# A fifth input tile of a routed convolution kernel: four block products, or three

## Chip, cores, metric

One core of one Trainium2 chip runs the kernel. The metric is the device time of one execution in microseconds (us), the median of several runs; lower is better.

## The reference

A grouped convolution of length 9 with a bias per sample and channel, then a router that picks 16 of 64 experts per row, and a low-rank layer whose 512 inner columns are weighted by the router:

```
h = conv1d(x, weight, pad 4, groups 4) + (c @ c_weight.T)[:, :, None] + bias     # x is (32, 64, 1024)
scores = (h @ Wq.T) @ keys.T                      # 64 scores of a row of 1024
gate = softmax of the 16 largest scores, 0 elsewhere
z = h @ A.T                                       # 512 = 64 experts x 8
out = x + 2.0 * (z * gate, expert by expert) @ B.T
```

## The kernel before

The 2048 rows are cut into 16 tiles of 128 rows: four tiles to each of the four channel groups, and eight samples to a tile. The program is written engine by engine. Each engine runs its own list of steps in the order of the code, and semaphores are the only thing that ties the lists together.

Every float32 product is made of three products of rounded parts. An operand has a high half (rounded, made on ACT by `high`, L509) and a low half (the rest, a subtraction on DVE by `low`, L1102, or in a few cases on GpSimd): high x high + high x low + low x high. A matmul of 512 columns is one TensorE instruction.

A tile t goes through these steps.

- Its input block is loaded (`load_blocks`), split into `x_hi` and `x_lo` (`split_x`), and convolved on TensorE into `p_conv`. The first five tiles (t < TW = 5) use the direct form, `conv` at L866: two output halves, two input blocks each, three products each, 12 matmuls. From tile TW on, the two halves share a product. DVE forms two differences of input blocks (`differ`, L1126), ACT splits the wider block of 1536 columns, TensorE makes 3 matmuls with the summed weights `ws` (`conv_sum`), ACT adds the bias and spreads the result over both halves in PSUM (`add_u_shared`, L559), and TensorE adds 3 matmuls to each half (`conv_pair`): 9 matmuls in all. `sum_w` and `split_ws` make the summed weights and their halves, once per channel group.
- ACT adds the bias (`add_u`, eight instructions, one a sample, into `h_c`) in the direct form. DVE transposes the rows into `h_t` (`turn_h`), and ACT and DVE split them (`split_h`: `h_hi`, `h_lo`).
- `z_product` multiplies by A and the query weights: 48 matmuls of 264 columns into two PSUM banks, `p_z` (tile 1: `p_out`). ACT takes the query (`take_q`), TensorE turns it, ACT copies it back (`copy_q`), TensorE makes the scores.
- DVE selects: `copy_scores`, `top_first`, `take_first`, `top_second`, `take_second`, `weigh`, `invert`, then `gate` in two instructions, which empties the banks of `p_z`, and `turn_z`. The gated z goes through DRAM and comes back transposed. `split_z` makes `zt_hi` and `zt_lo`.
- `out_high` (high and low z with `b_hi`) and `out_low` (high z with `b_lo`) make the output product, 24 matmuls of 512 columns for a tile, DVE adds x, and SP stores.

The weights B come in four chunks, c = 0 to 3. ACT makes `b_hi` of each, DVE the low halves of 1 to 3, and GpSimd that of 0 in four pieces of 256 columns (L499). `b_lo_done(c)` says which semaphore stands for a low half.

Buffers tie the steps together as well. While t < TW, the blocks lie in three slots of 1032 columns; later in two slots of 1544, over the same memory. So `load_blocks(t)` waits for the split of the tile that lay there. `x_hi`, `x_lo`, `h_hi` and `h_lo` have two slots each. `z_product(3)` needs the banks of `p_z`, so it waits for `gate(2)`.

The change touches the stretch from 22 to 50 us. TensorE finishes tile 2's z product and scores there, convolves tile 4 (L785), makes the output product of tile 0 (L933, L934, L941), and begins tile 3's z product (L892). The four lists were written out by hand for the first tiles, one call a line.

Of the kernel before, what the change touches and what calls it, by code (L numbers as in the profile page):

```python
# [14 lines left out]


NT = 16
TW = 5
TS = 4
FP = 6  # L20
NP = (NT - 2 - FP) // 2
# [24 lines left out]
def adaln_ffn(nc, x_blocks, x_rows, conv_w, a_wq, b_w, small, out):  # L46
# [13 lines left out]
    with ExitStack() as ctx:  # L60
# [197 lines left out]
        BP = 4  # L258
# [2 lines left out]
            return (s_wlop, 1) if g == 1 else (s_wlo, max(g, 1))  # L261

        def b_lo_done(c):
            return (s_blo, c) if c else (s_blop, BP)

        def x_lo_done(t, half=1):
            return s_xlo, x_split_count(t, half)
# [207 lines left out]
        @block.gpsimd  # L475
        def _(pool):
            nc.gpsimd.memset(ones, 1.0).then_inc(s_ones, 1)
            nc.gpsimd.memset(ident[:], 0.0).then_inc(s_iz, 1)
            nc.gpsimd.memset(q_w[:], 0.0).then_inc(s_qz, 1)
            nc.gpsimd.memset(q_t[:].bitcast(F32), 0.0).then_inc(s_qtz, 1)  # L480
            pool.wait_ge(s_iz, 1)
            nc.gpsimd.affine_select(out=ident[:], in_=ident[:], compare_op=ALU.not_equal, fill=1.0, base=0,
                                    pattern=[[-1, P]], channel_multiplier=1).then_inc(s_ident, 1)

            pool.wait_ge(s_cw, 1)
            nc.gpsimd.tensor_copy(cw[:, 2:NG], sm[:, SMALL_CW + 2 * CI:SMALL_CW + NG * CI].rearrange("d (g c) -> d g c", c=CI)
                                  .unsqueeze(2).to_broadcast([P, NG - 2, R, CI])).then_inc(s_cw, 1)

            pool.wait_ge(s_a[A_POOL], 16)
            nc.gpsimd.tensor_copy(a_hi[:, A_POOL, :], a_raw[:, A_POOL, :]).then_inc(s_ahp, 1)  # L490

            def split_w(g):
                pool.wait_ge(s_whi, g + 1)
                nc.gpsimd.tensor_tensor(w_lo[:, g % 2], w_raw[:, g], w_hi[:, g % 2].bitcast(F32), ALU.subtract).then_inc(s_wlop, 1)

            def split_b(c, piece):
                cols = slice(piece * L // BP, (piece + 1) * L // BP)
                pool.wait_ge(s_bhi, c + 1)
                nc.gpsimd.tensor_tensor(b_lo[:, c, cols], b_raw[:, c, cols], b_hi[:, c, cols].bitcast(F32),  # L499
                                        ALU.subtract).then_inc(s_blop, 1)  # L500

            split_w(1)
            for piece in range(BP):
                split_b(0, piece)

        @block.scalar
        def _(act):
# [65 lines left out]
            def split_b(c):  # L573
                act.wait_ge(s_b[c], 16)
                high(b_hi[:, c, :], b_raw[:, c, :], s_bhi)
# [79 lines left out]
            def copy_q(i):  # L655
                act.wait_ge(s_qtp, i + 1)
                high(q_f[:], p_conv[:, 2, 0:P], s_qt)
# [42 lines left out]
            add_u(3)  # L700
            exp(0)
            split_h(2)
            split_x(4)
            split_keys()
            take_q(1)
            split_w(1)
            copy_q(1)
            split_b(0)
            split_b(1)
            take_q(2)  # L710
            exp(1)
            copy_q(2)
            split_h(3)
            split_z(0)
            split_b(2)
            split_b(3)
            add_u(4)
            exp(2)
            sum_w(1)
            split_x(5)  # L720
            take_q(3)
            split_z(1)
# [53 lines left out]
        def _(pe):  # L776
# [89 lines left out]
            def conv(t):  # L866
                conv_direct(t, (0, 2, 1))
# [170 lines left out]
            z_product(2, 1, (0,), range(R // 2, R))  # L1038
            z_product(2, 2, (0,), range(R))
            scores(2)  # L1040
            conv(4)
            out_high(0, 0)
            out_high(0, 1)
            out_low(0, 0)
            out_low(0, 1)
            for i in range(3, NT):
# [53 lines left out]
        def _(dve):  # L1100
# [265 lines left out]
            gate(0)  # L1366
            turn_z(0)
            split_h(2)
            split_x(4)
            turn_h(3, 0)  # L1370
            turn_h(3, 1)
            copy_scores(1)
            top_first(1)
            take_first(1)
            top_second(1)
            split_b(1)
            take_second(1)
            weigh(1)
            invert(1)
# [11 lines left out]
            weigh(2)  # L1391
            invert(2)
            gate(2)
            sum_w(1)
            differ(5, 0)
            differ(5, 1)
            split_ws(1)
            turn_z(2)
            turn_h(4, 0)
            turn_h(4, 1)  # L1400
# [162 lines left out]
```

## Time and profile before

| | us |
|---|---|
| median of 3 runs (227.99 to 228.99) | 228.86 |
| profiled execution | 228.66 |
| its span, first to last instruction | 226.9 |
| TensorE busy with matmuls | 222.9 |
| DVE busy | 194.5 |
| ACT busy | 126.4 |
| GpSimd busy | 7.6 |

The span is what the trace covers; 1.8 us of the profiled execution lie around it. Busy time is a sum over instructions. Instructions of one engine overlap a little at their ends, so the time between two starts is the better measure of what one costs. All stamps below are us from the start of the span.

### The profile page before, as it was taken

To read this page: it belongs to the slowest core of one execution; us is meant where nothing else is said; L and a number is where in the kernel's file an instruction comes from. 1 tells how busy PE (TensorE), PEld (TensorE's weight loads), DVE (VectorE), ACT (ScalarE), POOL (GpSimd) and SP (SyncE) were. 2 spreads that over 40 slices of the span, in tenths; PEclk is the share of its full clock that TensorE was granted. 3 is DMA by queue.
4 is the path that set the end of the run, shared out by engine and by line. 5 is a ranking of instruction groups with operands and counts; after the bars stand their busy time and mean duration, and the time that the engine had idled before them with its cause. 6 is when DMAs were issued, how large, how long until landed. Compare 5 with 4: busy or idle time off the path is not lost.

```text
span 226.9 us, 4036 instructions
## 1 busy us (share of the span) xinstructions
PE 222.9 (98%) x1351; PEld 198.4 (87%) x1351; DVE 194.5 (86%) x443; ACT 126.4 (56%) x317; POOL 7.6 (3%) x16
## 2 busy tenths in 40 slices
PE   8999999999999999999999999999999999999995
PEld 6889998898988989889989889898998989898884
DVE  1799889999999989999999999899989995868442
ACT  4898857357274592936473856648473853252200
POOL 2010053000000000000000000000000000000000
PEclk9999999999999999999999999999999999999999
DMA  6997048659864666545261616655472337157642
GB/s 199 371 401 313 4 111 286 215 181 288 290 209 103 207 210 181 182 131 201 85 196 47 185 28 186 207 139 189 131 249 85 114 120 248 43 161 256 198 162 95
DMA packets 24869, 40.89 MB, mean 180 GB/s; under 512 B 2832, under 2 KB 11920, under 8 KB 24848
## 3 DMA queue, kind: packets, MB, share of 16 engines
q1 hardware_dynamic: 24704, 40.55, 55.4%
q8 instruction: 11, 0.18, 0.3%
q10 hardware_dynamic: 144, 0.08, 0.2%
q14 instruction: 10, 0.08, 0.1%
HBM read 28.04 MB, written 12.58 MB: 179 GB/s over the span
## 4 chain that ended last, share of the span: by engine, by line
PE 94%; DVE 3%; issue 1%; ACT 0%; POOL 0%; DVEq 0%; POOLq 0%
PE p_z L892 36%; PE p_conv L841 9%; PE p_out L933 6%; PE p_out L934 6%; PE p_out L941 6%; PE p_conv L785 5%; PE p_out L892 3%; PE p_out L961 3%; PE p_out L965 2%; PE p_out L963 2%; PE p_t L961 2%; PE p_conv L961 2%; PE p_t L963 2%; PE p_conv L965 2%; PE p_conv L963 2%; PE p_t L965 2%
## 5 line engine op out<-in xcount | busy, mean ns | idle before, releaser
L509 ACT ACTIVATE h_hi<-h_t 128x1024 fp32r<-128x1024 f32 x16 | 17.1, 1069 | 36.3 <-DVE h_t L1144 36.3
L892 PEld LDWEIGHTS p_z<-a_hi,h_hi 128*128 128x128 f32 x240 | 32.6, 188 | 2.1 <-DVE a_hi L1156 0.2
L892 PE MATMUL p_z<-a_hi,h_hi 128*128 128x264 f32 x240 | 34.2, 285 | 0.0
L892 PE MATMUL p_z<-a_hi,h_lo 128*128 128x264 f32 x240 | 34.1, 284 | 0.0
L892 PE MATMUL p_z<-a_lo,h_hi 128*128 128x264 f32 x240 | 33.9, 284 | 0.0
L892 PEld LDWEIGHTS p_z<-a_hi,h_lo 128*128 128x128 f32 x240 | 31.3, 188 | 0.2
L892 PEld LDWEIGHTS p_z<-a_lo,h_hi 128*128 128x128 f32 x240 | 31.0, 188 | 0.0
L1102 DVE TENSOR_TENSOR x_lo<-x_blk,x_hi 128x1536 fp32r<-128x1536 f32 (+4 forms) x18 | 25.3, 1406 | 2.3 <-ACT x_hi L509 2.2
L933 PE MATMUL p_out<-b_hi,zt_hi 128*128 128x512 f32 (+1 forms) x64 | 25.0, 393 | 0.0
L934 PE MATMUL p_out<-b_hi,zt_lo 128*128 128x512 f32 (+1 forms) x64 | 24.7, 388 | 0.0
L559 ACT ACTIVATE p_conv<-p_conv,u 128x128 f32<-128x128 f32 x88 | 23.7, 358 | 1.6 <-PE p_conv L841 1.4
L509 ACT ACTIVATE x_hi<-x_blk 128x1536 fp32r<-128x1536 f32 (+4 forms) x18 | 22.2, 1233 | 3.1 <-DMA x_blk<-in_x_blocks 2.0
L1102 DVE TENSOR_TENSOR h_lo<-h_t,h_hi 128x1024 fp32r<-128x1024 f32 x16 | 19.5, 1219 | 0.0
L941 PE MATMUL p_out<-b_lo,zt_hi 128*128 128x512 f32 (+1 forms) x64 | 16.9, 388 | 0.0
L1126 DVE TENSOR_TENSOR x_blk<-x_blk 128x512 f32<-128x512 f32 x22 | 15.0, 683 | 0.0
L1144 DVE STREAM_TRANSPOSE h_t<-p_conv 128x512 f32<-128x512 f32 x22 | 14.3, 688 | 0.0
L934 PEld LDWEIGHTS p_out<-b_hi,zt_lo 128*128 128x128 f32 x64 | 12.0, 188 | 2.5
L941 PEld LDWEIGHTS p_out<-b_lo,zt_hi 128*128 128x128 f32 x64 | 11.8, 188 | 2.7
L670 ACT ACTIVATE q_t<-q_c 32x32 fp32r<-32x32 f32 x48 | 11.0, 229 | 5.7 <-DVE q_c L1222 5.3
L933 PEld LDWEIGHTS p_out<-b_hi,zt_hi 128*128 128x128 f32 x64 | 12.0, 188 | 2.5
L1291 DVE SCALAR_TENSOR_TENSOR x_nat<-p_out,x_nat 128x512 f32<-128x512 f32 (+1 forms) x16 | 10.5, 657 | 4.0 <-PE p_out L941 4.0
L1273 DVE SCALAR_TENSOR_TENSOR a_raw<-p_z,e_inv,e_top 128x248 f32<-128x248 f32 (+1 forms) x30 | 13.1, 480 | 0.5
(160 smaller groups left out, 401.1 us busy)
## 6 DMA issues: line engine op xcount, KB each, us to landing
x_nat<-in_x_rows SPq DMA_DIRECT2D x16, 512.0 KB, 4.1
out_dram<-x_nat SPq DMA_DIRECT2D x31, 256.0 KB, 3.3
x_blk<-in_x_blocks SPq DMA_DIRECT2D x14, 516.0 KB, 3.8
z_dram<-a_raw SPq DMA_DIRECT2D x64, 64.0 KB, 1.8
a_raw<-z_dram SPq DMA_DIRECT2D x16, 256.0 KB, 2.9
a_raw<-in_a_wq SPq DMA_DIRECT2D x8, 264.0 KB, 6.5
x_nat<-in_b_w SPq DMA_DIRECT2D x4, 512.0 KB, 9.1
a_raw<-in_b_w SPq DMA_DIRECT2D x2, 512.0 KB, 5.1
```

Source lines behind the costliest of these rows:

```text
L509: nc.scalar.activation(dst, src, ACT.Copy).then_inc(s, 1)
L559: last = nc.scalar.activation(both[:, :, :, n], both[:, 1, :, n].unsqueeze(1).to_broadcast([P, 2, LK]), ACT.Identity, bias=u[:, t // TG, a ...
L841: mm = nc.tensor.matmul(dst, w, x[:, t % 2, part * XO:(part + 1) * XO], start=k == 0 and not onto, stop=k == 2, skip_group_check=onto)
L892: mm = nc.tensor.matmul(z_bank(t, b)[:, 0:HB], h[:, t % 2, r, :], a[:, r, b * HB:(b + 1) * HB], start=k == 0 and r == 0, stop=k == 2 and r ...
L933: nc.tensor.matmul(dst, zt_hi[:, block, c % 2, :], b_hi[:, c, cols], start=c == 0, stop=False)
L934: nc.tensor.matmul(dst, zt_lo[:, block, c % 2, :], b_hi[:, c, cols], start=False, stop=False)
L941: mm = nc.tensor.matmul(dst, zt_hi[:, zt_first(t) + c // 2, c % 2, :], b_lo[:, c, start:stop], start=False, stop=c == JC - 1)
L961: nc.tensor.matmul(dst, zt_hi[:, block, c, :], high[:, c, :], start=c == 0 and not onto, stop=False, skip_group_check=onto)
L963: nc.tensor.matmul(dst, zt_lo[:, block, c, :], high[:, c, :], start=False, stop=False, skip_group_check=onto)
L1102: nc.vector.tensor_tensor(dst, src, hi.bitcast(F32), ALU.subtract).then_inc(s, 1)
L1126: nc.vector.tensor_tensor(blocks[:, NN:XE] if ab else blocks[:, XS:XW], blocks[:, ab * NN:ab * NN + XO], blocks[:, XE:XS], ALU.subtract).t ...
L1144: nc.vector.transpose(dst, src).then_inc(s_tr, 1)
```

## The change

Tile 4 is convolved in the shared form: TW is 4. The three matmuls of `conv_sum(4)` stand where `conv(4)` stood, and the six of `conv_pair(4)` behind the two high parts of tile 0's output product. `sum_w(1)`, `split_ws(1)` and the two differences of tile 4 move forward on DVE, and the low half of B's chunk 1 moves from DVE to GpSimd, behind that of chunk 0. On ACT, tile 4's additions, now the shared form, stand ahead of `split_h(3)`.

```diff
-TW = 5
+TW = 4
...
         def b_lo_done(c):
-            return (s_blo, c) if c else (s_blop, BP)
+            return (s_blop, BP * (c + 1)) if c < 2 else (s_blo, c - 1)
...
 (gpsimd)
             split_w(1)
-            for piece in range(BP):
-                split_b(0, piece)
+            for c in range(2):
+                for piece in range(BP):
+                    split_b(c, piece)
...
 (scalar)
             split_h(2)
-            split_x(4)
             split_keys()
             take_q(1)
             split_w(1)
             copy_q(1)
+            split_x(4)
+            sum_w(1)
             split_b(0)
-            split_b(1)
             take_q(2)
             exp(1)
             copy_q(2)
-            split_h(3)
+            split_b(1)
             split_z(0)
             split_b(2)
             split_b(3)
-            add_u(4)
+            add_u_shared(4)
+            split_h(3)
             exp(2)
-            sum_w(1)
...
 (tensor)
             scores(2)
-            conv(4)
+            conv_sum(4)
             out_high(0, 0)
             out_high(0, 1)
+            conv_pair(4)
             out_low(0, 0)
             out_low(0, 1)
...
 (vector)
             split_h(2)
-            split_x(4)
+            differ(4, 0)
+            differ(4, 1)
+            sum_w(1)
             turn_h(3, 0)
             turn_h(3, 1)
             copy_scores(1)
             top_first(1)
             take_first(1)
             top_second(1)
-            split_b(1)
+            split_x(4)
+            split_ws(1)
             take_second(1)
...
             gate(2)
-            sum_w(1)
             differ(5, 0)
             differ(5, 1)
-            split_ws(1)
```

How the lists read in the built programs follows for the two places where TensorE's operands come from. The line numbers of the changed kernel differ by one or two.

ACT, from the copy of tile 2's query (`q_f`) to the exponentials of tile 2 (`e_all`). `h_c<-p_conv,u` is `add_u(4)`, `p_conv<-p_conv,u` the shared form. Before:

```order
L509 ACTIVATE q_f<-p_conv 128x128
L509 ACTIVATE h_hi<-h_t 128x1024
L509 ACTIVATE zt_hi<-a_raw 128x512
L509 ACTIVATE b_hi<-x_nat 128x1024 x2
L545 ACTIVATE h_c<-p_conv,u 128x128 x8
L680 ACTIVATE e_all<-sc,neg_max 128x64
```

And of the change:

```order
L510 ACTIVATE q_f<-p_conv 128x128
L510 ACTIVATE b_hi<-x_nat 128x1024
L510 ACTIVATE zt_hi<-a_raw 128x512
L510 ACTIVATE b_hi<-x_nat 128x1024 x2
L560 ACTIVATE p_conv<-p_conv,u 128x128 x8
L510 ACTIVATE h_hi<-h_t 128x1024
L681 ACTIVATE e_all<-sc,neg_max 128x64
```

`h_hi` of tile 3 stood first behind the query and now stands last; a third `b_hi`, chunk 1, has come to its place.

DVE, from the second maximum of tile 1 (`top_b`) to the scores of tile 2 (`sc<-p_z`). Before:

```order
L1252 MAX top_b<-sc_a 128x8
L1102 TENSOR_TENSOR b_lo<-x_nat,b_hi 128x1024
L1256 MATCH_REPLACE sc_b<-top_b,sc_a 128x64
L1261 SCALAR_TENSOR_TENSOR e_top,e_sum<-sc_b,e_all 128x64
L1266 RECIPROCAL e_inv<-e_sum 128x1
L1273 SCALAR_TENSOR_TENSOR a_raw<-p_out,e_inv,e_top 128x248
L1273 SCALAR_TENSOR_TENSOR a_raw<-p_out,e_inv,e_top 128x264
L1283 STREAM_TRANSPOSE a_raw<-a_raw 128x4x4x32
L1102 TENSOR_TENSOR zt_lo<-a_raw,zt_hi 128x512
L1102 TENSOR_TENSOR h_lo<-h_t,h_hi 128x1024
L1229 COPY sc<-p_z 128x64
```

And of the change:

```order
L1254 MAX top_b<-sc_a 128x8
L1104 TENSOR_TENSOR x_lo<-x_blk,x_hi 128x1536
L1104 TENSOR_TENSOR ws_lo<-ws_raw,ws_hi 128x128
L1258 MATCH_REPLACE sc_b<-top_b,sc_a 128x64
L1263 SCALAR_TENSOR_TENSOR e_top,e_sum<-sc_b,e_all 128x64
L1268 RECIPROCAL e_inv<-e_sum 128x1
L1275 SCALAR_TENSOR_TENSOR a_raw<-p_out,e_inv,e_top 128x248
L1275 SCALAR_TENSOR_TENSOR a_raw<-p_out,e_inv,e_top 128x264
L1285 STREAM_TRANSPOSE a_raw<-a_raw 128x4x4x32
L1104 TENSOR_TENSOR zt_lo<-a_raw,zt_hi 128x512
L1104 TENSOR_TENSOR h_lo<-h_t,h_hi 128x1024
L1231 COPY sc<-p_z 128x64
```

`b_lo` of chunk 1 is gone from here; tile 4's `x_lo`, now of 1536 columns, and `ws_lo` have come to its place. `h_lo` of tile 3 still stands ahead of all that tile 2's selection needs.

## Rows read from the trace of the kernel before

**Rows 1.** The page: engines' busy time, granted clock by slice, engines in the chain of waits.

```profile
PE 222.9 (98%) x1351; PEld 198.4 (87%) x1351; DVE 194.5 (86%) x443; ACT 126.4 (56%) x317; POOL 7.6 (3%) x16
...
PEclk9999999999999999999999999999999999999999
...
PE 94%; DVE 3%; issue 1%; ACT 0%; POOL 0%; DVEq 0%; POOLq 0%
```

**Rows 2.** Timeline of TensorE: start, duration, engine, line, operation, tiles, count.

```profile
35.98 1.17 PE L785 MATMUL p_conv<-x_hi,w_hi 128*128 128x512 f32 x4
...
38.84 0.39 PE L933 MATMUL p_out<-b_hi,zt_hi 128*128 128x512 f32 x1
...
44.44 1.14 PE L892 MATMUL p_z<-a_hi,h_hi 128*128 128x264 f32 x8
```

**Rows 3.** Timeline of DVE; in brackets an idle time and what ended it.

```profile
21.11 1.19 DVE L1102 TENSOR_TENSOR x_lo<-x_blk,x_hi 128x1032 fp32r<-128x1032 f32 x1
...
29.66 1.22 DVE L1102 TENSOR_TENSOR x_lo<-x_blk,x_hi 128x1032 fp32r<-128x1032 f32 x1
...
33.53 0.23 DVE L1252 MAX8 top_b<-sc_a 128x8 f32<-128x64 f32 x1 [0.57 <-DVE sc_a L1248]
33.68 1.66 DVE L1102 TENSOR_TENSOR b_lo<-x_nat,b_hi 128x1024 fp32r<-128x1024 f32 x1
...
35.58 0.45 DVE L1261 SCALAR_TENSOR_TENSOR e_top<-sc_b,e_all 128x64 f32<-128x64 f32 x1
...
37.81 0.65 DVE L1102 TENSOR_TENSOR zt_lo<-a_raw,zt_hi 128x512 fp32r<-128x512 f32 x1
38.38 1.22 DVE L1102 TENSOR_TENSOR h_lo<-h_t,h_hi 128x1024 fp32r<-128x1024 f32 x1
...
40.02 1.21 DVE L1102 TENSOR_TENSOR b_lo<-x_nat,b_hi 128x1024 fp32r<-128x1024 f32 x1
...
41.28 0.21 DVE L1248 MATCH_REPLACE8 sc_a<-top_a,sc 128x64 f32<-128x64 f32 x1
41.63 0.23 DVE L1252 MAX8 top_b<-sc_a 128x8 f32<-128x64 f32 x1
...
43.22 0.23 DVE L1261 SCALAR_TENSOR_TENSOR e_top<-sc_b,e_all 128x64 f32<-128x64 f32 x1
...
43.68 0.88 DVE L1273 SCALAR_TENSOR_TENSOR a_raw<-p_z,e_inv,e_top 128x248 f32<-128x248 f32 x2
44.48 0.28 DVE L1114 TENSOR_TENSOR ws_raw<-w_raw 128x128 f32<-128x128 f32 x1
44.67 1.41 DVE L1126 TENSOR_TENSOR x_blk<-x_blk 128x512 f32<-128x512 f32 x2
...
48.02 1.72 DVE L1102 TENSOR_TENSOR x_lo<-x_blk,x_hi 128x1536 fp32r<-128x1536 f32 x1
```

**Rows 4.** Timeline of ACT.

```profile
34.77 1.05 ACT L509 ACTIVATE h_hi<-h_t 128x1024 fp32r<-128x1024 f32 x1
35.72 0.62 ACT L509 ACTIVATE zt_hi<-a_raw 128x512 fp32r<-128x512 f32 x1
36.24 2.00 ACT L509 ACTIVATE b_hi<-x_nat 128x1024 fp32r<-128x1024 f32 x2
...
51.28 2.16 ACT L559 ACTIVATE p_conv<-p_conv,u 128x128 f32<-128x128 f32 x8 [1.40 <-PE p_conv L841]
```

**Rows 5.** Instructions of GpSimd's line L499: duration in ns, min/median/max; first and last start.

```profile
L499 POOL TENSOR_TENSOR b_lo<-x_nat,b_hi x4: 737/741/1722, 32.1 to 34.2; 128x256 fp32r<-128x256 f32 x4
```

**Rows 6.** Waits of TensorE's weight loads: us in total, times, longest us.

```profile
PEld p_z L914 <- ACT q_t L670: 0.8, 3, 0.4
```

**Rows 7.** The page, DMA issues: count, KB each, median us to landing.

```profile
x_blk<-in_x_blocks SPq DMA_DIRECT2D x14, 516.0 KB, 3.8
```

**Rows 8.** Instructions of line L793, TensorE's first passes: duration in ns, first and last start.

```profile
L793 PE MATMUL p_z<-sm,h_t x8: 275/407/422, 4.1 to 5.5; 128*128 128x100 f32 x8
```

## The prediction

> **What bounds the kernel now.** I read the shares of the engines and the chain of waits first [rows 1]. TensorE is busy for 222.9 of the 226.9 us and makes up 94% of the chain that ended last, at a granted clock of full speed, the 2.4 GHz level, in every slice. So a matmul less is time less, as long as TensorE finds its operands ready. DVE, at 86%, is close behind, so the second question is always whether TensorE has to wait for DVE. The timeline of TensorE answers that for the kernel before [rows 2]: the fifth tile's direct convolution starts at 35.98, the output product of tile 0 at 38.84, the query and gate product of tile 3 (called z(3) here) at 44.44, with no gap. 24 matmuls of 512 columns lie between 38.84 and 44.44: 0.233 us each.
>
> The timelines of DVE and ACT give the margins at those two places [rows 3, 4]. The output product needs tile 0's low half zt_lo: DVE ends it at 37.81 + 0.65 = 38.46, 0.4 us before TensorE asks. z(3) needs the first of gate(2)'s two instructions, which ends at 43.68 + 0.44 = 44.12, 0.3 us before. So TensorE leads by nothing and follows by little: whatever makes TensorE faster here, or DVE slower, shows up at once as a wait.
>
> **What is removed on TensorE.** The direct form of tile 4 has 12 matmuls, the new one 3 + 6 = 9. Three at 0.233 are 0.70 us. That is the whole direct gain: z(3) would start at 43.74 if nothing else moved. 0.70 us is 0.3% of the time, and about 0.5%, 1.14 us, is what a measurement of this kernel can tell from no change.
>
> **Where TensorE now arrives.** Only 3 of the 9 matmuls stay ahead of the output product, so TensorE reaches it at 35.98 + 0.70 = 36.7 instead of 38.84, that is 2.1 us earlier, with zt_lo at 38.46 even if DVE kept its pace. From the start S of the output product to z(3) there are now 16 + 6 + 8 = 30 matmuls, 7.0 us. The change breaks even only if S is no later than 44.44 - 7.0 = 37.4.
>
> **DVE up to zt_lo.** DVE's instructions overlap by some 0.09 where they follow each other (0.28 from 44.48, the next at 44.67 [rows 3]), so I take that off each. Ahead of turn_h(3) come the two differences, 1.41 - 0.09 = 1.32, and sum_w, 0.19; x_lo(4), 1.13, goes away from there. Behind the second maximum, b_lo(1), 1.57, is replaced by the longer x_lo(4) of 1536 columns, 1.63, and ws_lo, of sum_w's form, 0.19. In sum 1.32 + 0.19 - 1.13 + 1.63 + 0.19 - 1.57 = +0.63: zt_lo ends at 39.1.
>
> **GpSimd beside it.** The four pieces of b_lo(0) do not run for free [rows 3, 5]. While they run, DVE stands idle 0.57 ahead of its second maximum (0.14 in the next tile, 41.49 to 41.63, so 0.43 is lost), b_lo(1) takes 1.66 where b_lo(2) takes 1.21, and the weighting at 35.58 takes 0.45 where the next tile's takes 0.23. One piece takes 1.72 us where the median is 0.74, so the two engines hold each other up. The loss of DVE is 0.43 + 0.45 + 0.22 = 1.10 for four pieces, 0.28 each. 39.1 carries 0.65 of it, the part outside b_lo(1). Eight pieces at that price lose 2.2, which is 1.55 more: zt_lo ends at 40.65. The bounds: 38.45 with no loss at all; and if each of the four DVE instructions ahead of S that read two tiles (x_lo(4), ws_lo, the weighting, zt_lo) waited for a whole piece, 0.69 from start to start [rows 5] (three steps from 32.1 to 34.2), 38.45 + 2.8 = 41.2. I take 40.65, since the rows show the same instruction beside the same kind of DVE work. Then S is 40.7 and z(3) can start at 47.7; at the bounds 45.5 and 48.3.
>
> The Trainium skill (SBUF — State Buffer, "Who interferes with whom") says that a DVE instruction with two SBUF inputs and a GpSimd instruction that reads SBUF exclude each other, and that the second to issue blocks until the first is finished. By it the upper bound is the likely case, and the sum would be that of rival (c). The long b_lo(1) and the long piece agree with the rule; the idle 0.57 ahead of a maximum, which has one input, is more than it says.
>
> **ACT up to z(3).** This is a second wait, and it does not depend on GpSimd. Before, ACT makes h_hi(3) at 34.77 [rows 4]. Now it stands behind b_hi(1), zt_hi, b_hi(2), b_hi(3) and the eight shared additions of tile 4. From the same point: 0.95 for b_hi(1) (34.77 to 35.72, the same form), 0.52 for zt_hi, 2.00 less 0.1 of overlap for the two others, 2.16 for the eight additions (tile 5's row at 51.28), then 1.05 for h_hi(3): 34.77 + 0.95 + 0.52 + 1.9 + 2.16 + 1.05 = 41.35. DVE's queue has h_lo(3) ahead of all the selection of tile 2, so it waits there: h_lo(3) starts at 41.4 instead of 38.38, 3.0 later. copy_scores(2), b_lo(2), b_lo(3) and gate(2) follow as before, so gate(2)'s first half ends at 47.1 and z(3) starts at 47.2; up to 47.8 if GpSimd's last two pieces each hold up a DVE instruction (2 x 0.28).
>
> **The sum.** z(3) starts at the later of 47.7 (zt_lo, then 30 matmuls) and 47.2 to 47.8 (h_hi(3), then DVE). I take 47.5, 3.1 us after 44.44; the three matmuls saved are inside. Behind it DVE is rid of sum_w and ws_lo, 0.4 us, and TensorE's three later waits for the query, 0.8 us together [rows 6], can shrink: between 0 and 0.8, I take 0.2, as DVE's margin at z(3) also falls from 0.3 to 0.1. The sum is +2.9. The profiled execution took 228.66 us (span 226.9, 1.8 around it), 0.2 below the median 228.86, so 228.66 + 2.9 = **231.6 us**.
>
> **Costed at nothing.** Tile 4's load now waits for x_lo(3), which ends at 22.3 [rows 3], and lands about 3.8 us later [rows 7], at 26.1; the differences want it at 29.7. If that cover of 3.6 us went, DVE would wait. On SP's queue, load 6 waits for the later x_lo(4), with tile 0's rows and the store of z(1) behind it; both wait for DVE and GpSimd longer anyway. Tile 1's rows wait for GpSimd's eighth piece, near 42, and are used some 20 us later. What GpSimd makes of b_lo(1) is read by the second matmul of the low part, 23 x 0.233 behind S, near 46. turn_h(4) now reads PSUM after the pair, which ends 1.9 us before z(3).
>
> **The rivals.** (a) *Not slower*: the move to GpSimd is worth more than I count. Its place is DVE between the second maximum and zt_lo, where b_lo(1), 1.57, and the 0.65 of hold-ups go; if x_lo(4) and the differences fell into gaps, TensorE would run through, and 228.66 - 0.70 = 228.0 results, 0.3% faster, which counts as no change. It decides at S: zt_lo must end by 37.4, and h_hi(3) by 38.5. Against: DVE's rows show no gaps of that size, even without any loss to GpSimd they give 38.45, and 41.35 for h_hi(3). 7%, with partial versions up to 229.8. (b) *DVE alone*: h_hi(3) is earlier than I add up, or ACT overlaps more, and only the lighter S holds, 38.45 to 39.1: z(3) at 45.5 to 46.2, 229.7 to 230.4. 8%. (c) *DVE and GpSimd exclude each other fully*: the upper bound 41.2, z(3) at 48.3, 3.8 late, less 0.2 behind it: 232.3. The 1.66 and the 1.72 of [rows 3, 5] speak for it, the average of 0.28 a piece against it. 15%. (d) *The clock*: TensorE stands still for 3 to 4 us, which it never does in the trace of before. The only passes that ran at the lower level are those before 5.5 us: the 100-column pass has a median of 407 ns there, and 275 for the fastest, the last of them [rows 8], a factor 1.5. If half of the 30 matmuls (3.5 us) ran at a factor 1.5 to 2, 1.7 to 3.5 us are added: some 234. The granted clock is full in all 40 slices [rows 1], so nothing here shows it. 8%. (e) The late load of tile 4 misses 29.7 by a microsecond: 232.6. 3%.
>
> The Trainium skill (TensorE: Matmul & The Clock Gate, "Part 1: The HAM clock gate") says that the array falls back to 1.2 GHz after it has been idle; rival (d) is that rule at work, and no run here shows it yet.
>
> **How the numbers follow.** My forecast, with z(3) 2.2 to 3.8 us later, has 59%, and with (c) and (e), which lie in the same range or beside it, 77%. The range 230.2 to 233.5 holds these, part of (b) and the mild end of (d): some 82%. Faster by over 0.5% would need 1.14 us where at most 0.70 are saved: 2%. Within 0.5%, below 230.0: (a) and half of (b), 10%. Slower: 88%.
>
> **What would show it.** In the timeline of TensorE: a wait ahead of the output product, S near 40.7, and z(3) near 47.5. On ACT h_hi(3) at 40.3 behind the eight additions; on DVE h_lo(3) at 41.4 right behind it, and stretched two-input instructions from 34 to 42; behind z(3) the two traces run in parallel, apart by about 3 us. Wrong is all this if TensorE shows no idle stretch between 36 and 48, if z(3) starts before 45, or if the distance at z(3) is given back by the end.

## The result, and the profile after

The changed kernel takes 231.95 us in the median of 4 runs (231.66 to 232.77), against 228.62 us for the kernel before in the median of 4 runs beside it (227.99 to 228.99). The ratio is 1.016, with a 95% interval of 1.014 to 1.019: slower by 3.3 to 4.2 us. The forecast was 231.6 us, in a range of 230.2 to 233.5.

The profiled execution took 232.77 us; its span is 231.0 us. The page of the changed kernel, the same three lines as [rows 1]:

```profile
PE 224.4 (97%) x1348; PEld 199.5 (86%) x1348; DVE 196.5 (85%) x444; ACT 126.2 (55%) x317; POOL 10.8 (5%) x20
...
PEclk9999999799999999999999999999999999999999
...
PE 77%; DVE 13%; issue 3%; ACT 3%; DMA 2%; SPq 1%; DVEq 0%; ACTq 0%
```

TensorE runs three matmuls less and yet is busy 1.5 us longer, and one slice of the clock line shows a 7. TensorE has 77% of the chain, where it had 94%; DVE has risen from 3% to 13%.

The program reaches the changed stretch at a moment that differs by more than a microsecond between executions: the scores of tile 2, the last thing that TensorE does ahead of that stretch in both kernels, start at 35.0 to 36.3 us in the profiles of this study. Distances from that point are steadier than stamps. So I measure from scores(2), which in the kernel before is this row of TensorE's timeline:

```profile
35.84 0.33 PE L914 MATMUL p_z<-sm,q_f 128*128 128x64 f32 x2
```

S came 3.00 behind it and z(3) 8.60 (38.84 and 44.44 in [rows 2]). The timeline of TensorE in the changed kernel:

```profile
36.27 0.33 PE L915 MATMUL p_z<-sm,q_f 128*128 128x64 f32 x2
37.03 0.47 PE L842 MATMUL p_conv<-x_hi,ws_hi 128*128 128x512 f32 x1 [0.43 <-issue]
...
40.23 0.47 PE L934 MATMUL p_out<-b_hi,zt_hi 128*128 128x512 f32 x1 [2.27 <-DVE zt_lo L1104]
...
42.25 0.63 PE L934 MATMUL p_out<-b_hi,zt_hi 128*128 128x512 f32 x1
42.67 0.63 PE L935 MATMUL p_out<-b_hi,zt_lo 128*128 128x512 f32 x1
...
45.12 0.40 PE L934 MATMUL p_out<-b_hi,zt_hi 128*128 128x512 f32 x1
45.35 0.39 PE L935 MATMUL p_out<-b_hi,zt_lo 128*128 128x512 f32 x1
...
48.85 1.15 PE L893 MATMUL p_z<-a_hi,h_hi 128*128 128x264 f32 x8
```

TensorE waits 2.27 us for zt_lo; S is 3.96 behind scores(2). Then something new happens: from 41 to 44.5 us the starts of the 512-column matmuls lie 0.42 to 0.43 apart (42.25 to 42.67), before and after it 0.23 (45.12 to 45.35). The view by stretches says what that is (its columns: the stretch, its length, the busy time and count of TensorE, its weight loads, DVE, ACT and GpSimd, then the granted clock, the share of the DMA engines and GB/s):

```profile
38.00:40.20 2.20, 0.00 (x0) 0.00 (x0) 2.10 (x4) 2.20 (x8) 2.20 (x4) 1.00 0.62 204
40.20:41.05 0.85, 0.81 (x4) 0.71 (x5) 0.00 (x0) 0.85 (x3) 0.85 (x2) 1.00 0.80 246
41.05:44.46 3.41, 3.41 (x10) 2.63 (x9) 2.63 (x4) 0.60 (x1) 1.06 (x2) 0.50 0.49 159
44.46:47.00 2.54, 2.54 (x13) 2.05 (x12) 2.36 (x10) 0.35 (x1) 0.00 (x0) 1.00 1.08 329
```

The granted clock is 0.50 from 41.05 to 44.46, the 1.2 GHz level; it fell 0.8 us after TensorE had come back to work. z(3) starts at 48.85, 12.58 behind scores(2) where it was 8.60: 3.98 us later. From there the two traces run in parallel: from z(3) to the end of the span it is 182.5 us before and 182.2 after. Of the 0.3 given back, 0.2 goes with a wait for the query that is gone; of the three [rows 6] two are left, 0.6 us together.

A small part of the cost lies ahead of scores(2), where this measure does not see it. From the first matmul of z(2) to scores(2) it is 6.30 us before (29.54 to 35.84) and 6.47 after (29.80 to 36.27). The list of waits of the changed kernel has the difference (us in total, times, longest): TensorE now waits for ACT, which makes a `b_hi` ahead of tile 2's query.

```profile
PEld p_conv L905 <- ACT q_w L510: 0.2, 1, 0.2
```

DVE in the changed kernel, the rows that answer to [rows 3]:

```profile
29.94 1.82 DVE L1128 TENSOR_TENSOR x_blk<-x_blk 128x512 f32<-128x512 f32 x2
...
34.31 0.23 DVE L1254 MAX8 top_b<-sc_a 128x8 f32<-128x64 f32 x1
34.46 1.74 DVE L1104 TENSOR_TENSOR x_lo<-x_blk,x_hi 128x1536 fp32r<-128x1536 f32 x1
36.11 0.82 DVE L1104 TENSOR_TENSOR ws_lo<-ws_raw,ws_hi 128x128 fp32r<-128x128 f32 x1
...
37.16 0.45 DVE L1263 SCALAR_TENSOR_TENSOR e_top<-sc_b,e_all 128x64 f32<-128x64 f32 x1
...
39.40 0.74 DVE L1104 TENSOR_TENSOR zt_lo<-a_raw,zt_hi 128x512 fp32r<-128x512 f32 x1
41.68 1.52 DVE L1104 TENSOR_TENSOR h_lo<-h_t,h_hi 128x1024 fp32r<-128x1024 f32 x1 [1.55 <-ACT h_hi L510]
...
47.28 0.88 DVE L1275 SCALAR_TENSOR_TENSOR a_raw<-p_z,e_inv,e_top 128x248 f32<-128x248 f32 x2
```

The differences are 0.41 longer than in [rows 3], ws_lo takes 0.82 where its form takes 0.28 (ws_raw there), and DVE stands idle 1.55 us for h_hi(3). The timeline of ACT, to be read beside [rows 4]:

```profile
35.17 1.05 ACT L510 ACTIVATE b_hi<-x_nat 128x1024 fp32r<-128x1024 f32 x1
36.12 0.62 ACT L510 ACTIVATE zt_hi<-a_raw 128x512 fp32r<-128x512 f32 x1
36.64 1.99 ACT L510 ACTIVATE b_hi<-x_nat 128x1024 fp32r<-128x1024 f32 x2
38.54 2.13 ACT L560 ACTIVATE p_conv<-p_conv,u 128x128 f32<-128x128 f32 x8
40.54 1.11 ACT L510 ACTIVATE h_hi<-h_t 128x1024 fp32r<-128x1024 f32 x1
```

h_hi(3) stands last, as the lists had it, and ends at 41.65; gate(2)'s first half follows at 47.28 + 0.44 = 47.72. The instructions of GpSimd's line L499, beside [rows 5]:

```profile
L499 POOL TENSOR_TENSOR b_lo<-x_nat,b_hi x8: 722/732/2192, 34.6 to 41.4; 128x256 fp32r<-128x256 f32 x8
```

Eight pieces where there were four, with one of 2.19 us among them.

### The profile page after: what moved, and what is told of

The parts are those of the page before. It is cut to its first block, busy times and chain, and to the rows that moved or that the text cites. A ratio compares the mean times of both kernels' runs of the same rounds, so it can differ in the third digit from the quotient of the medians.

```text
span 231.0 us, 4035 instructions
## 1 busy us (share of the span) xinstructions
PE 224.4 (97%) x1348; PEld 199.5 (86%) x1348; DVE 196.5 (85%) x444; ACT 126.2 (55%) x317; POOL 10.8 (5%) x20
## 3 DMA queue, kind: packets, MB, share of 16 engines
HBM read 28.04 MB, written 12.58 MB: 176 GB/s over the span
## 4 chain that ended last, share of the span: by engine, by line
PE 77%; DVE 13%; issue 3%; ACT 3%; DMA 2%; SPq 1%; DVEq 0%; ACTq 0%
PE p_z L893 30%; PE p_conv L842 10%; PE p_out L934 6%; PE p_out L935 6%; PE p_out L942 6%; PE p_out L962 2%; PE p_out L964 2%; PE p_out L966 2%; DMA x_blk<-in_x_blocks 2%; DVE a_lo L1104 2%; DVE x_lo L1104 2%; PE p_t L962 2%; PE p_conv L962 2%; DVE h_t L1146 2%; PE p_t L964 2%
## 5 line engine op out<-in xcount | busy, mean ns | idle before, releaser
L934 PE MATMUL p_out<-b_hi,zt_hi 128*128 128x512 f32 (+1 forms) x64 | 26.0, 409 | 2.3 <-DVE zt_lo L1104 2.3
L1104 DVE TENSOR_TENSOR x_lo<-x_blk,x_hi 128x1536 fp32r<-128x1536 f32 (+4 forms) x18 | 25.8, 1435 | 2.5 <-ACT x_hi L510 2.5
L560 ACT ACTIVATE p_conv<-p_conv,u 128x128 f32<-128x128 f32 x96 | 25.8, 357 | 1.6 <-PE p_conv L842 1.4
L935 PE MATMUL p_out<-b_hi,zt_lo 128*128 128x512 f32 (+1 forms) x64 | 25.6, 402 | 0.0
L934 PEld LDWEIGHTS p_out<-b_hi,zt_hi 128*128 128x128 f32 x64 | 12.6, 197 | 5.3 <-issue 2.7
L1128 DVE TENSOR_TENSOR x_blk<-x_blk 128x512 f32<-128x512 f32 x24 | 16.7, 698 | 0.1
L1146 DVE STREAM_TRANSPOSE h_t<-p_conv 128x512 f32<-128x512 f32 x24 | 15.6, 686 | 0.0
L935 PEld LDWEIGHTS p_out<-b_hi,zt_lo 128*128 128x128 f32 x64 | 12.6, 197 | 2.7
```

The source lines that it names most:

```text
L560: last = nc.scalar.activation(both[:, :, :, n], both[:, 1, :, n].unsqueeze(1).to_broadcast([P, 2, LK]), ACT.Identity, bias=u[:, t // TG, a ...
L934: nc.tensor.matmul(dst, zt_hi[:, block, c % 2, :], b_hi[:, c, cols], start=c == 0, stop=False)
L935: nc.tensor.matmul(dst, zt_lo[:, block, c % 2, :], b_hi[:, c, cols], start=False, stop=False)
L1104: nc.vector.tensor_tensor(dst, src, hi.bitcast(F32), ALU.subtract).then_inc(s, 1)
L1128: nc.vector.tensor_tensor(blocks[:, NN:XE] if ab else blocks[:, XS:XW], blocks[:, ab * NN:ab * NN + XO], blocks[:, XE:XS], ALU.subtract).t ...
L1146: nc.vector.transpose(dst, src).then_inc(s_tr, 1)
```

## The experiments

The trace offers four readings. **Theory A**: z(3) starts at the later of two times, S plus the 30 matmuls (7.0 us, 1.6 more where the clock falls), and gate(2), which hangs on h_hi(3). Of the two, only the later one costs time. **B**: the late h_hi(3) alone is the cost. **C**: the fall of the clock is paid in full. **D**: what counts is that GpSimd and DVE hold each other up, by 1.5 us or more.

All kernels start from the changed one, but for the fifth, which starts from the kernel before. The table has them together: distances in us, each from one profiled execution; the median is of four to twelve executions; the ratio is to runs of the kernel before on the same chip (medians 228.2 to 228.6).

| kernel | S behind scores(2) | z(3) behind scores(2) | z(3) to end of span | median us | ratio, 95% interval |
|---|---|---|---|---|---|
| before | 3.00 | 8.60 | 182.5 | 228.62 | 1 |
| changed | 3.96 | 12.58 | 182.2 | 231.95 | 1.016 (1.014 to 1.019) |
| 1 h_hi(3) early | 3.98 | 12.59 | 182.1 | 232.51 | 1.015 (1.012 to 1.019) |
| 2 clock kept | 4.04 | 11.72 | 182.2 | 231.83 | 1.015 (1.012 to 1.017) |
| 3 both | 4.01 | 11.07 | 182.2 | 230.97 | 1.010 (1.008 to 1.013) |
| 4 b_lo(1) on DVE | 3.88 | 12.48 | 182.4 | 232.30 | 1.017 (1.014 to 1.020) |
| 5 before, b_lo(1) on GpSimd | 2.99 | 8.59 | 182.2 | 228.34 | 1.000 (0.998 to 1.001) |
| 6 differences on GpSimd | 3.51 | 12.04 | 182.2 | 231.71 | 1.014 (1.011 to 1.017) |
| 7 and weights' sum early | 3.34 | 11.94 | 182.1 | 231.94 | 1.014 (1.012 to 1.017) |
| 8 GpSimd held back | 3.15 | 11.76 | 184.9 | 234.07 | 1.024 (1.022 to 1.026) |
| 9 b_lo(0), b_lo(1) early | 3.47 | 10.55 | 182.1 | 231.06 | 1.013 (1.011 to 1.016) |
| 10 and clock kept | 3.59 | 10.56 | 182.2 | 230.55 | 1.011 (1.009 to 1.013) |
| 11 best order | 2.77 | 9.94 | 182.2 | 229.86 | 1.008 (1.005 to 1.010) |

**1. h_hi(3) early.** ACT makes h_hi(3) where the kernel before made it.

```diff
 (scalar)
             copy_q(2)
+            split_h(3)
             split_b(1)
...
             add_u_shared(4)
-            split_h(3)
```

> The change, with tile 3's high half h_hi(3) back on ACT right behind the copy of tile 2's query. Theory A (z(3) starts at the later of two things: the output product's start S plus 30 matmuls, 7.0 us plus 1.6 us where the clock is low; and gate(2), which hangs on h_hi(3)): in the changed kernel 40.2 + 8.6 = 48.8 is already the later, gate(2) is ready near 47.8, so with the clock still falling nothing is gained: 231.7 to 232.0 us. Theory B (the late h_hi(3) is what costs): 1 to 3 us less, 229 to 231 us. In both DVE starts h_lo(3) behind zt_lo near 40.1 and not at 41.7.

z(3) stays 12.59 behind scores(2), though h_lo(3) now starts right behind zt_lo and gate(2) is early: its first half ends at 45.71 + 0.44 = 46.15, and z(3) starts at 48.62.

```profile
45.71 0.88 DVE L1275 SCALAR_TENSOR_TENSOR a_raw<-p_z,e_inv,e_top 128x248 f32<-128x248 f32 x2
```

The time, 232.51, is even a little above the 231.7 to 232.0 expected. B falls: h_hi(3), which the change makes 5.3 us later against scores(2), costs nothing as long as TensorE's own path is the longer one. Where the clock holds, that path is the shorter one: of the six executions of this kernel one kept a mean granted clock of 1.000 and took 230.49 us, the five others took 232.08 to 235.49.

**2. Clock kept.** Ten matmuls whose result nobody reads fill TensorE's wait.

```diff
 (tensor)
             conv_sum(4)
+            for _ in range(10):
+                nc.tensor.matmul(p_t[:], a_hi[:, 0, 0:P], a_hi[:, 0, 0:512], start=True, stop=True)
             out_high(0, 0)
```

> The change, with ten matmuls of 512 columns that nobody reads put into TensorE's wait ahead of the output product (2.3 us, the length of that wait). Theory A: the granted clock stays at its upper level, the output product's 16 matmuls take 3.7 us and not 5.4, and z(3) moves from 48.8 to where gate(2) lets it start, 47.8: 1.0 us less, 230.9 us. Theory B (h_hi(3) alone costs, the clock hides under it): no gain, 231.9 us. Theory C (the fall of the clock is paid in full): 1.6 us less, 230.3 us. If the wait were not idle time after all, ten matmuls would cost 2.3 us: 234.2 us.

The view by stretches of this kernel shows a granted clock (third number from the end) of 1.00 throughout:

```profile
36.00:40.30 4.30, 3.81 (x19) 2.85 (x18) 4.08 (x11) 4.30 (x11) 4.30 (x6) 1.00 0.51 145
40.30:44.00 3.70, 3.68 (x16) 3.02 (x17) 2.15 (x4) 1.37 (x3) 1.90 (x3) 1.00 0.63 194
44.00:48.00 4.00, 3.64 (x17) 2.48 (x15) 3.75 (x13) 0.35 (x1) 0.00 (x0) 1.00 0.86 287
```

z(3) comes 0.86 earlier, not 1.6: C falls. The rest waits for DVE, whose work still hangs on h_hi(3). TensorE meets that wait ahead of gate(2): the low part of the output product needs b_lo(3), which DVE makes behind h_lo(3).

```profile
46.73 1.43 PE L942 MATMUL p_out<-b_lo,zt_hi 128*128 128x512 f32 x5 [0.36 <-DVE b_lo L1106]
```

Five matmuls of 0.233 from 46.73 lead to 47.90, and gate(2)'s first half ends at 47.81; z(3) starts at 48.00. So the second path of theory A enters by b_lo(3) and by gate(2) within 0.1 us of each other. The 0.86 is read from one profile. The median, 231.83, is not the 230.9 that A expected, and beside the changed kernel's 231.95 it shows no gain: the two intervals overlap.

**3. Both.** The two edits together.

> The two edits together. Theory A: z(3) starts at S + 7.0 = 47.2, 1.6 us earlier than in the changed kernel: 230.3 us, and the two edits give more together than the sum of each alone. Theory B: the same as h_hi(3) early alone. Theory C: the same as the kept clock alone.

z(3) comes 1.51 earlier, more than the sum of the two alone (0 and 0.86), and here the times agree: 230.97, against 232.51 and 231.83 for each edit alone on the same chip. That is what two parallel paths look like: A. With both remedies the change still costs 2.6 us in the median, since S is still 4.0 behind scores(2).

**4. b_lo(1) back on DVE**, behind zt_lo; GpSimd makes chunk 0 alone.

```diff
 (gpsimd)
-            for c in range(2):
-                for piece in range(BP):
-                    split_b(c, piece)
+            for piece in range(BP):
+                split_b(0, piece)
...
 (vector)
             split_z(0)
+            split_b(1)
             split_h(3)
```

> The change, with b_lo(1) back on DVE, between zt_lo and h_lo(3), where DVE stands idle for 1.55 us; GpSimd makes chunk 0 alone. Theory A: of what GpSimd takes from DVE only the small part of its second four pieces goes (0.1 ahead of S, 0.3 in h_lo(3)): 231.5 to 231.9 us. Theory D (sharing between GpSimd and DVE is the main cost of the change, 1.5 us and more): at least 1.2 us less, 230.7 us or below.

z(3) moves by 0.1 us, and the time, 232.30, does not fall. Put into DVE's idle time behind zt_lo, the second chunk is worth next to nothing either way.

**5. The kernel before, with b_lo(1) on GpSimd alone.**

```diff
 (gpsimd)
-            for piece in range(BP):
-                split_b(0, piece)
+            for c in range(2):
+                for piece in range(BP):
+                    split_b(c, piece)
...
 (vector)
             top_second(1)
-            split_b(1)
             take_second(1)
```

> The kernel before (five tiles in the direct form, 12 matmuls for tile 4) with one part of the change alone: b_lo(1) is made by GpSimd behind b_lo(0), in eight pieces in place of four, and DVE no longer makes it. Theory A (GpSimd's sharing is small, and TensorE's own work is the bound there): DVE reaches zt_lo earlier or at the same time, TensorE does not wait ahead of the output product, z(3) lies 8.6 us after scores(2) as in the kernel before, time within 0.5 us of the kernel before, 228.3. Rival D (eight pieces hold DVE up by 1.5 us or more): zt_lo after 39, a wait of TensorE ahead of the output product, z(3) 9.5 us or more after scores(2), time 229.3 or more.

Equal, with 228.34 us and an interval that holds 1. D falls for this part. DVE does lose time here too, as its timeline in this kernel shows:

```profile
34.13 0.81 DVE L1262 SCALAR_TENSOR_TENSOR e_top<-sc_b,e_all 128x64 f32<-128x64 f32 x1
...
36.72 0.78 DVE L1103 TENSOR_TENSOR zt_lo<-a_raw,zt_hi 128x512 fp32r<-128x512 f32 x1
```

The weighting takes 0.81 and zt_lo 0.78 (0.45 and 0.65 in [rows 3]), but zt_lo ends at 37.50 and TensorE asks at 38.73.

**6 and 7. Tile 4's differences and the sum of the weights on GpSimd**, with h_hi(3) early; then also the halves of the summed weights ahead of the stretch.

```diff
 (gpsimd)
+            sum_w(1)
+            differ(4, 0)
+            differ(4, 1)
             split_w(1)
...
 (vector)
-            differ(4, 0)
-            differ(4, 1)
-            sum_w(1)
             turn_h(3, 0)
```

The seventh kernel against the sixth:

```diff
 (scalar)
             split_keys()
+            sum_w(1)
             take_q(1)
...
             split_x(4)
-            sum_w(1)
...
 (vector)
+            split_ws(1)
             turn_h(3, 0)
...
             split_x(4)
-            split_ws(1)
```

> The changed kernel with h_hi(3) made ahead of the b_hi of chunk 1, as in the first experiment, and in addition tile 4's two differences and the sum of the weights made by GpSimd in place of DVE, ahead of its b_lo pieces. Theory A (what counts is when zt_lo comes, and h_hi(3) is out of the way): DVE gets rid of 1.82 + 0.2 us ahead of zt_lo, the start S of the output product comes from 3.96 us after scores(2) to some 2.0 to 2.6, z(3) 9.0 to 9.6 us after scores(2) if the clock holds in the shorter wait, up to 1.0 more if it falls; time 228.7 to 230.5. Rival D (DVE and GpSimd hold each other up, so work moved to GpSimd costs DVE as much as it saves): S stays 3.5 us or more after scores(2), time 231 or more.

> As the kernel with the differences on GpSimd, and the high half of the summed weights made on ACT before the first b_hi, their low half on DVE ahead of turn_h(3), so that conv_sum(4) does not wait for ws_lo and DVE has one instruction less between the second maximum and zt_lo. Theory A: S 1.5 to 2.5 us after scores(2) and z(3) 8.5 to 9.5 us after it, against 8.6 in the kernel before; time 228.0 to 229.5, so no more than equal to the kernel before. Rival D: S 3.5 us or more after scores(2), time 231 or more. If z(3) comes less than 8.6 us after scores(2), this beats the kernel before by up to 0.7 us.

Both missed: S came 3.51 and 3.34 behind scores(2), not 2.0 to 2.6 and 1.5 to 2.5. There are two reasons. DVE, rid of 2 us, ran into a wait for the scores of tile 1 (0.44 in the sixth kernel), so that only 0.7 of the 2 us arrived. And on the way from there to zt_lo it lost time at other places: without ws_lo behind it, x_lo(4) took the hold-up by GpSimd, and DVE stood idle ahead of the second maximum, as its timeline in the seventh kernel shows.

```profile
33.82 0.23 DVE L1270 MAX8 top_b<-sc_a 128x8 f32<-128x64 f32 x1 [0.56 <-DVE sc_a L1266]
33.97 2.21 DVE L1120 TENSOR_TENSOR x_lo<-x_blk,x_hi 128x1536 fp32r<-128x1536 f32 x1
```

The idle 0.56 is not GpSimd's doing; the last section comes back to it. Here GpSimd's first piece started at 33.81, ahead of x_lo(4); in the changed kernel x_lo(4) was first, at 34.46 against 34.59, and took 1.74, and the long piece, 2.19, was on GpSimd's side. The Trainium skill (SBUF — State Buffer, "Who interferes with whom") says that the order of issue decides which of the two blocks; these two rows agree.

**8. GpSimd held back until zt_lo is made**, b_lo(1) on DVE as in the fourth.

```diff
 (gpsimd)
+            pool.wait_ge(s_ztlo, 1)
             for piece in range(BP):
                 split_b(0, piece)
```

> The changed kernel with b_lo(1) back on DVE (behind zt_lo, ahead of h_lo(3)), and GpSimd held back until zt_lo is made, so that nothing runs on GpSimd while DVE goes from the second maximum to zt_lo. It prices the sharing of the four pieces on the way to zt_lo. Theory A (small price): ws_lo falls from 0.8 to about 0.3, the weighting from 0.45 to 0.23, S comes 0.8 us earlier, about 3.1 us after scores(2) in place of 3.9; z(3) some 11.3 to 11.7 after scores(2), time about 231. Rival D (1.5 us or more): S 2.4 us or less after scores(2), z(3) bound by h_hi(3) alone, at about 11 us, time below 230.5.

The timeline of DVE in this kernel:

```profile
34.95 0.28 DVE L1104 TENSOR_TENSOR ws_lo<-ws_raw,ws_hi 128x128 fp32r<-128x128 f32 x1
...
35.47 0.23 DVE L1263 SCALAR_TENSOR_TENSOR e_top<-sc_b,e_all 128x64 f32<-128x64 f32 x1
...
37.48 0.65 DVE L1104 TENSOR_TENSOR zt_lo<-a_raw,zt_hi 128x512 fp32r<-128x512 f32 x1
```

The price on the way to zt_lo is settled: against the changed kernel's rows it is 0.54 on ws_lo, 0.22 on the weighting and 0.09 on zt_lo, and S comes 0.73 earlier than in the fourth. z(3) is 11.76 behind scores(2), a little above what was expected, but the time was missed by 3 us. Behind z(3) this kernel loses 2.7. SP's queue in the changed kernel, then in this one:

```profile
38.93 0.33 SPq L364 DMA_DIRECT2D x_nat<-in_x_rows  x1
39.50 1.77 SPq L399 DMA_DIRECT2D z_dram<-a_raw  x4
```

```profile
44.01 0.33 SPq L364 DMA_DIRECT2D x_nat<-in_x_rows  x1
44.39 1.90 SPq L399 DMA_DIRECT2D z_dram<-a_raw  x4
```

In the code the load of tile 0's rows waits for GpSimd's last piece of chunk 0, and the write of z(1) stands behind it on SP. Both come 5 us later. Some 24 to 39 us further on TensorE has waits that the changed kernel does not have, in its timeline:

```profile
67.70 0.33 PE L915 MATMUL p_z<-k_r,q_t 128*128 128x128 f32 x1 [0.30 <-ACT q_t L671]
72.84 0.51 PE L934 MATMUL p_out<-b_hi,zt_hi 128*128 128x512 f32 x1 [0.57 <-DVE x_nat L1293]
83.27 0.33 PE L915 MATMUL p_z<-k_r,q_t 128*128 128x128 f32 x1 [0.84 <-ACT q_t L671]
```

They are 1.7 of the 2.7 us. That the queue is the cause is read from the code and the stamps; it was not tried with another order on SP. This kernel bears on theory A as well, since h_hi(3) is late in it: two of its four executions kept a mean granted clock of 1.000 and took 234.08 and 234.18 us, no less than the two at 0.993 (233.55 and 234.06).

**9 and 10. b_hi and b_lo of chunks 0 and 1 some 5 us earlier**, added to the seventh; the tenth also has four matmuls that nobody reads behind `conv_sum(4)`.

```diff
 (scalar)
             sum_w(1)
+            split_b(0)
+            split_b(1)
             take_q(1)
...
             split_x(4)
-            split_b(0)
...
-            split_b(1)
...
 (gpsimd)
-            split_w(1)
             for c in range(2):
                 for piece in range(BP):
                     split_b(c, piece)
+            split_w(1)
```

> As the kernel with the differences on GpSimd and the summed weights' halves early, and in addition ACT makes the high halves of B's chunks 0 and 1 some 5 us earlier, ahead of tile 1's query, and GpSimd its low halves right behind, ahead of w_lo of the second channel group. So GpSimd's eight pieces run from about 29 to 35 and not beside DVE's way from the second maximum to zt_lo. Theory A: that way gets shorter by the 0.5 of idle time ahead of the maximum, the 0.5 of the long x_lo(4), 0.2 of the weighting and 0.1 of zt_lo; S comes from 3.3 to 2.0 to 2.6 us after scores(2), z(3) 9.0 to 9.6 us after scores(2) if the clock holds and up to 1.6 later if it falls; time 228.7 to 230.5, still no better than the kernel before, where z(3) lies 8.6 us after scores(2). Rival (the hold-ups go along with GpSimd's work wherever it stands, and delay DVE's start of this way by as much): S 3.0 us or more after scores(2).

> The kernel of the run beside it, with four matmuls of 512 columns that nobody reads behind conv_sum(4) (0.93 us at the full clock), which shorten TensorE's wait ahead of the output product. If the clock falls in the run beside it, this one should keep it and bring z(3) forward by up to 1.6 us, to some 9.0 to 9.6 us after scores(2); if the clock holds there, nothing changes. Time 228.7 to 229.7.

The ninth's S is 3.47 behind scores(2), not 2.0 to 2.6, so the number of its rival came out, though only a part of it is GpSimd's. The eight pieces lasted from 28.40 to 36.56. x_lo(4) took 2.22 and the weighting 0.44 beside them, and further ahead h_lo(2) 1.44 and ws_lo 0.82, where they take 1.18 and 0.28 alone. DVE stood idle 0.56 ahead of the maximum as in the seventh. A second miss was mine: `conv_sum(4)` also waits for w_lo, which I had put behind the pieces. TensorE's timeline in the ninth kernel:

```profile
37.61 0.47 PE L858 MATMUL p_conv<-x_hi,ws_hi 128*128 128x512 f32 x1 [1.57 <-POOL w_lo L494]
...
39.19 0.47 PE L950 MATMUL p_out<-b_hi,zt_hi 128*128 128x512 f32 x1 [0.64 <-issue]
```

But in the profiled execution the clock held, and z(3) came 7.08 behind S. Executions of this one kernel show what the clock is worth: the three whose mean granted clock was 1.000 took 230.32, 230.38 and 230.63 us, the three at 0.993 took 231.50, 231.98 and 232.12. That is 1.6 us between their middles. In the tenth, with the four extra matmuls, all six stayed at 0.999 or above; five took 230.40 to 230.75, one 231.95, so the clock is not the only thing that differs between executions. The tenth's z(3) and its median, 10.56 and 230.55, missed what was expected too, for S was no earlier.

**11. The best order found**: the ninth, with b_lo(0) alone on GpSimd and w_lo behind it, b_lo(1) on DVE behind zt_lo.

```diff
 (scalar)
             split_b(0)
-            split_b(1)
             take_q(1)
...
             split_z(0)
+            split_b(1)
             split_b(2)
...
 (gpsimd)
-            for c in range(2):
-                for piece in range(BP):
-                    split_b(c, piece)
+            for piece in range(BP):
+                split_b(0, piece)
...
 (vector)
             split_z(0)
+            split_b(1)
             split_h(3)
```

> The most that the runs so far point to, still with tile 4 in the shared form: the differences and the summed weights on GpSimd, h_hi(3) early, b_lo(0) on GpSimd early (about 28.5 to 32.5) with w_lo behind it, b_lo(1) on DVE behind zt_lo. So nothing runs on GpSimd while DVE goes from the second maximum to zt_lo, and conv_sum(4) need not wait for w_lo. Theory A: DVE's second maximum without the idle 0.56, x_lo(4) 1.75 in place of 2.22, the weighting 0.23 in place of 0.44; S 2.2 to 2.6 us after scores(2), z(3) at the later of S + 7.0 and DVE's gate(2), 9.2 to 9.7 us after scores(2), against 8.6 in the kernel before and 12.6 in the changed one; the clock holds. Time 228.7 to 229.6, equal to the kernel before or 0.3% above. Rival (the hold-ups by GpSimd only move): S 3.3 us or more after scores(2), z(3) at 10.3 or more, time above 229.8.

The timeline of DVE in this kernel:

```profile
33.78 0.23 DVE L1269 MAX8 top_b<-sc_a 128x8 f32<-128x64 f32 x1 [0.56 <-DVE sc_a L1265]
33.93 1.74 DVE L1119 TENSOR_TENSOR x_lo<-x_blk,x_hi 128x1536 fp32r<-128x1536 f32 x1
...
35.90 0.22 DVE L1278 SCALAR_TENSOR_TENSOR e_top<-sc_b,e_all 128x64 f32<-128x64 f32 x1
```

S is 2.77 behind scores(2), a little above the 2.2 to 2.6 expected: x_lo(4) and the weighting are short again, but DVE stood idle 0.56 ahead of the maximum as before, though GpSimd's last instruction, w_lo, had ended at 33.13. z(3) is 9.94 behind scores(2): 1.34 late, and the time is 1.4 us above the kernel before. Both lie a little above what was expected; the clock held in the profile, but two of the six executions were at 0.993. No version beat the kernel before. To do so, S would have to come within 1.6 us of scores(2) (8.60 less 7.0); the best was 2.77. An order in which TensorE does something else between `conv_sum(4)` and S was not tried.

## Why the prediction was right, and where it was not

The direction and the size were right, the mechanism in its main line too: TensorE arrives early, waits for DVE, and what follows keeps its distance. Two terms were off by nearly a microsecond each, in opposite directions. In the same measure (behind scores(2), 35.84 in the kernel before):

| step | predicted | measured |
|---|---|---|
| h_hi(3) ends on ACT | 5.5 | 5.4 |
| S | 4.9 | 3.96 |
| S to z(3), 30 matmuls | 7.0 | 8.62 |
| gate(2), first half | 11.3 | 11.45 |
| z(3) | 11.7 | 12.58 |
| given back behind z(3) | 0.2 | 0.3 |

- **DVE up to zt_lo, and GpSimd beside it.** zt_lo ended 2.62 behind scores(2) before and 3.87 after, 1.25 later; I had 2.2. The part without GpSimd, +0.63, stands. The term that was mis-sized is GpSimd's price of 0.28 a piece, 1.55 for four more pieces. Of the 1.10 that this price was read from, the 0.43 ahead of the maximum was not GpSimd's: the idle time stands in kernels in which GpSimd did nothing at that moment (the last section). Measured, the change adds 0.41 on the differences (beside w_lo, which I had not counted), 0.54 on ws_lo and 0.09 on zt_lo, and takes away 0.31 ahead of the maximum (1.51 from copy_scores(1) to it before, 1.20 after): 0.73. With 0.63 that is 1.36. Counted from the start of h_lo(2), zt_lo ended 9.90 behind it before the change and 11.30 after, so DVE is 1.40 later; by that count scores(2) itself is 0.15 later, which leaves the 1.25. With the 0.30 on h_lo(3) and the 0.22 on the weighting the eight pieces cost DVE 0.14 each. The full exclusion of rival (c) asked for S at 41.2 or 5.4; it did not come.
- **From S to z(3).** The sum took 30 matmuls at the full clock, and gave the fall of the clock 8%. That step failed: the clock fell in all four timed executions (mean granted clock 0.993 in each). The Trainium skill (TensorE: Matmul & The Clock Gate, "Part 1: The HAM clock gate") says that an idle array falls back to 1.2 GHz; the stretch at 0.50 agrees as to the level, though it began only after TensorE was at work again. Its price was smaller than rival (d) had it, which let half of the 30 matmuls run slowly: here it was eight, 0.43 apart and not 0.23. On TensorE's own path they and their ends cost 1.6, but DVE would have held z(3) back anyway, and the second experiment's profile shows 0.86.
- **ACT up to z(3).** Right to 0.2 us, and of no effect by itself, as the first experiment shows; it became the longer path only where the clock held, and there TensorE met it at b_lo(3) as soon as at gate(2).
- **TensorE's arrival.** `conv_sum(4)` started 0.76 behind scores(2) in place of 0.14; ws_lo ended only at 36.93, and with ws_lo early, in the seventh kernel, it is 0.14 again. I had not counted that wait; it costs nothing as long as zt_lo is later still.
- **What was costed at nothing.** Tile 4's late load did no harm: the differences started at 29.94, right behind h_lo(2). SP's queue did none either in this kernel, but the eighth experiment shows what stands behind it.

The sum itself had a slip: the later of 47.7 and 47.2 to 47.8 is at least 47.7, and I took 47.5. The two errors offset each other: with S right and the clock held the sum would have been 0.3 lower (gate(2) at 11.3 then decides), and with my S and the slow clock it would have been above 233. So 231.6 beside 231.95 is closer than its working deserves.

The three matmuls saved, 0.70 us, never showed. S would have to be early enough to cash them in, and the direct form's nine other matmuls had covered DVE's way to zt_lo.

## What to carry to other kernels

Removing work from the engine that bounds the kernel pays only as far as its next operand is ready: read the margin of that operand first (0.4 us here), and compare it with how much earlier the engine will ask (2.1 us). Where two waits end at the same point, taking one away shows nothing; take both away before calling either harmless. A pause of TensorE can cost more than its own length, since the matmuls behind it may run at the lower clock: here a wait of 2.27 us was followed by eight such matmuls, 1.6 us more.

## What was not expected of the hardware

- After a wait of 2.27 us TensorE's granted clock fell to 0.50 although it was already at work again: 0.8 us after its return in the changed kernel, 41.05 to 44.46. In the sixth experiment it fell just before TensorE came back at 39.27, which its view by stretches shows (0.98 up to 39.20, 0.51 from there):

```profile
36.00:39.20 3.20, 0.98 (x4) 0.48 (x3) 3.06 (x9) 2.94 (x4) 3.20 (x5) 0.98 0.64 197
39.20:42.60 3.40, 3.33 (x8) 2.69 (x9) 3.25 (x7) 2.29 (x9) 3.40 (x3) 0.51 0.67 213
42.60:45.00 2.40, 2.40 (x11) 1.91 (x11) 2.15 (x9) 0.35 (x1) 0.51 (x1) 1.00 0.49 181
```

- Whether it falls differs between executions of one kernel. In the sixth experiment one of six executions kept a mean clock of 1.000 and took 230.17 us, the other five, at 0.993, took 231.54 to 232.47.
- DVE's idle 0.56 ahead of its second maximum ([rows 3], the fifth, seventh, ninth, tenth and eleventh kernels) is not a hold-up by GpSimd, as the prediction took it. In the seventh kernel the maximum started at 33.82 behind 0.56 of idle time; GpSimd had been idle for 2.58 us until its first piece:

```profile
33.81 9.51 POOL L499 TENSOR_TENSOR b_lo<-x_nat,b_hi 128x256 fp32r<-128x256 f32 x8 [2.58 <-ACT b_hi L526]
```

What the idle time does follow is the place in DVE's list. Counted with its semaphore instructions, the 64th instruction that the trace records of DVE is late in all thirteen profiles. It is the second maximum in the six kernels named. In the sixth it is x_lo(4), with 0.21 of idle time ahead of it. In the changed kernel and in the first four and the eighth, whose lists have two instructions more ahead of the maximum, it is the MATCH_REPLACE before the maximum, which loses some 0.1. In the kernel before an idle time of the same kind stands ahead of the 192nd, long after GpSimd's last instruction (at 35.9):

```profile
79.69 0.23 DVE L1243 MAX8 top_a<-sc 128x8 f32<-128x64 f32 x1 [0.52 <-DVE sc L1231]
```

What happens at these places stays open.
